# A decoder layer in two halves: early loading of the second half's weights, another order for its first batch, normalisations moved to ScalarE

## The chip, the cores and the metric

The kernel runs on one core of a Trainium2 chip. The metric is the device time of one execution in microseconds (us), as the median of several executions. The engines are TensorE (PE), VectorE (DVE), ScalarE (ACT), GpSimd (POOL) and SyncE (SP, which here only starts DMAs).

## The reference

For 16 batches of 100 rows of 512 numbers the layer computes three steps, each added to its input:

```
x = x + self_attention(layernorm(x))       # 64 heads of 32 in four windowed branches
x = x + cross_attention(layernorm(x), ctx) # 16 heads of 32, 722 context rows, top 32 scores per query
x = x + real(ifft(fft(layernorm(x)) @ w))  # as one 512x512 matrix, plus a bias
```

In the cross attention the scores are `q k / sqrt(32)`; of each query's 722 scores only the 32 largest enter the softmax, and their weights multiply the projected values. Keys and values are projections of the context (`ctx @ Wk.T + bk`, `ctx @ Wv.T + bv`). All is float32. The third step's matrix M is worked out on the chip from the spectral weights.

## The kernel before, in words

The program has two halves, each a block of five instruction streams with its own semaphores; the second starts when all engines have ended the first.

**First half** (`self_program`, L105 to L649): self attention. Each engine runs `body` for the batches -2 to 16, a software pipeline in which `cur`, `prev`, `nxt` and `far` switch stages on. While a batch's scores are computed, the q and k projections of the next one are made with the weights `WqkH` and `WqkL`, which fill the lowest part of SBUF. In the body of batch 15 nothing more is projected to q and k. SP stores `x1` to HBM (L241) and loads the residual `xres` (L239). At its end the mean row `y3` is written to HBM (L244).

**Second half** (`cross_program`, L680 to L1423): cross attention and the spectral step. It begins with a preparation:

- SP loads the signs, four folded spectral matrices and a DFT matrix in four chunks of 128 rows (L862 to L867), then the eight 128x512 pieces of the key and value weights (L869), the first half of the context (L880), the rest of the weights (`SETUP`, L886) and, after GpSimd's 16 accumulating DMAs of L912 have landed (`x1_whole`), the first batch's rows (L894).
- DVE folds each chunk (L1330, L1338), TensorE multiplies it with the DFT matrix (L1027), ACT copies the product out (L1191), and TensorE multiplies again (L1034), which ACT copies to `M` (L1305).
- ACT and DVE split the key and value weights into a high and a low part (L1195, L1349), so that three fast matmuls (`split3`, L88 to L90) stand for one exact product.

Then come the batches. A batch has 13 score tiles: 12 of 128 rows (four heads' queries for 32 numbers each, packed) and one of 64. They are worked through in seven steps, s = 0 to 6, two tiles in each and one in the last. For a tile TensorE makes the scores (`score`, into one PSUM buffer `pS`), ACT copies them to SBUF (`keep_scores`, L1246), and DVE picks the top 32: MAX8 of the scores (L1362), MATCH_REPLACE8 of the eight found (L1381), then three rounds of the same on what is left (L1372, L1384). ACT exponentiates what was there (L1239) and what was left (L1229), GpSimd subtracts (L950), TensorE transposes (L1091) and multiplies with the values (L1120, L1124). GpSimd also makes the softmax shift (L942).

Beside a batch's tiles the keys and values of the next batch are made, in 14 slices: `SLICES` lists for each half of the context four key slices and three value slices, `PLAN` says at which step each is projected by TensorE (`project`), kept by ACT (`keep`, L1215, L1219, L1221) and, for keys, given its low part by GpSimd (`key_low`, L927). Before the first batch the same plan runs with no tiles beside it. The context itself is split by ACT (L1206) and GpSimd (L935).

Two normalisations belong to a batch. At s = 0 DVE takes the statistics of the next batch's rows (`row_stats`, L95 to L97), GpSimd the inverse deviation (L997), and DVE normalises (L1394). At s = 3 DVE adds the attention's output in PSUM to the residual (L1405), takes its statistics, GpSimd makes the inverse deviation (L1000), and at s = 4 DVE normalises (L1412). Later TensorE multiplies by `M` (L1143) and DVE adds (L1417).

`settle` (L59) issues a no-operation; it stands behind many waits.

Of the kernel before, what the change touches and what calls it, by code (L numbers as in the profile page):

```python
# [17 lines left out]
F32 = mybir.dt.float32  # L18
# [86 lines left out]
def self_program(nc, A, x1_dram, y3_dram):  # L105
# [10 lines left out]
    with ExitStack() as ctx:  # L116
# [108 lines left out]
        def _(sp):  # L225
# [6 lines left out]
            def body(b, cur, prev, nxt, far):  # L232
# [447 lines left out]
def cross_program(nc, A, x1_dram, y3_dram, out_dram):  # L680
# [16 lines left out]
    assert [n for a, b in PLAN[1:] + PLAN[:1] for n in a + b] == list(range(NSL))  # L697
    with ExitStack() as ctx:
# [3 lines left out]
        chunks = lambda t, n: t.rearrange("p (c d) -> p c d", c=n)  # L702
        M = sb("M", [128, CC, D])
        WkH, WkL, WvH, WvL = (sb(n, [128, CC, D], F32R) for n in ("WkH", "WkL", "WvH", "WvL"))
# [10 lines left out]
        SLOT = [128, KV]  # L715
        KH, K32, KL, V, S = [None, None], [None, None], [None, None], [None, None], [None] * SLOTS

        def own(p):

            KH[p] = sb(f"KH{p}", [128, CC, KV], F32R)  # L720
            with ExitStack() as below:
                K32[p] = below.enter_context(nc.sbuf_tensor(f"ca_K32{p}", [128, CC, KV], F32))
            KL[p] = sb(f"KL{p}", [128, CC, KV], F32R)
            V[p] = sb(f"V{p}", [128, KC, D])

        own(0)
        with ExitStack() as below:
            fold = {n: below.enter_context(nc.sbuf_tensor(f"ca_fold_{n}", [128, CC, D], F32)) for n in FOLDS}
            dft = below.enter_context(nc.sbuf_tensor("ca_dft", [128, CC, D], F32))
            signs = below.enter_context(nc.sbuf_tensor("ca_signs", [128, CC, 4, 2], F32))  # L730
        folded, spread = fold["pp"], fold["mp"]
        own(1)
        for r in (4, 5, 6, 0, 1, 2, 3):
            S[r] = sb(f"S{r}", SLOT)

# [4 lines left out]
        W = [sb(f"W{r}", [128, KV]) for r in range(RING)]  # L740
# [6 lines left out]
        stats, mv, rstd = sb("stats", [T, 6]), sb("mv", [T, 2]), sb("rstd", [T, 1])  # L747
# [739 lines left out]
```

## Time and profile before

| | us |
|---|---|
| median of 3 runs (2321.08 to 2322.66) | 2322.45 |
| the profiled execution's own time | 2323.47 |
| its span | 2321.6 |
| DVE busy in the span | 1950.9 (84%) |
| PE busy in the span | 2076.8 (89%) |
| ACT busy | 1266.3 (55%) |
| POOL busy | 1277.2 (55%) |

Times in the rows below are us from the start of the span; the profiled execution's own time is 1.9 us more than its span, and 1.0 us more than the median. In a row of a timeline stand the start, the time from the start of the first to the end of the last instruction of the row, the engine, the line, the operation, the tiles, the shapes and the count; in brackets how long the engine was idle before it and what ended that. A row with `x2` or more merges that many instructions of one kind. SPq rows are DMA issues of SP's queue. PE's granted clock is given as a share of 2.4 GHz.

### The profile page before, as it was taken

What the parts mean: (1) busy time and instruction counts of PE and PEld (TensorE: products, weight loads), DVE (VectorE), ACT (ScalarE), POOL (GpSimd) and SP (SyncE); (2) the same over time, 40 slices, a digit from 0 to 9 for tenths busy, and PEclk for the clock granted to TensorE, in tenths of its full rate; (3) what the DMA queues carried; (4) which work ended last, traced back from release to release, by engine and by line L of the source; (5) the groups of instructions that cost most, each with busy time, mean ns of one, the idle gap of its engine ahead of it and who ended that gap; (6) DMA issues with size and microseconds to landing.
All of it is one profiled execution on the core that took longest, in us unless ns stands there. A gap on an engine that the chain in (4) does not pass through costs nothing. (4 is left out here: it accounts for less than half of the span.)

```text
span 2321.6 us, 50944 instructions
## 1 busy us (share of the span) xinstructions
PE 2076.8 (89%) x19760; PEld 1627.4 (70%) x19760; DVE 1950.9 (84%) x3662; ACT 1266.3 (55%) x2464; POOL 1277.2 (55%) x1473
## 2 busy tenths in 40 slices
PE   2899999999957889999999999999999999999966
PEld 1566666666644778787787787887878778788754
DVE  4757676676722499999999999999999999999995
ACT  4333333333312476766666666766666766666652
POOL 2555646465641465656556656556556655665642
PEclk9999999999968899999999999999999999999977
DMA  5000000000036100000001000010000000100000
GB/s 190 12 16 20 16 23 13 23 13 26 9 82 191 30 19 13 30 26 21 18 21 38 19 20 25 13 37 18 20 26 23 28 18 21 37 18 21 8 1 11
DMA packets 41501, 70.42 MB, mean 30 GB/s; under 512 B 4639, under 2 KB 21167, under 8 KB 41261
## 3 DMA queue, kind: packets, MB, share of 16 engines
q1 hardware_dynamic: 35868, 56.31, 7.8%
q0 software_dynamic: 3632, 7.58, 1.4%
q10 hardware_dynamic: 1760, 3.28, 0.5%
q8 instruction: 157, 2.57, 0.5%
q14 instruction: 84, 0.68, 0.1%
HBM read 60.54 MB, written 9.86 MB: 30 GB/s over the span
## 5 line engine op out<-in xcount | busy, mean ns | idle before, releaser
L1384 DVE MATCH_REPLACE8 ca_W<-ca_top,ca_W 128x722 f32<-128x722 f32 (+1 forms) x624 | 553.1, 892 | 0.0
L1372 DVE MAX8 ca_top<-ca_W 128x8 f32<-128x722 f32 (+1 forms) x624 | 536.8, 897 | 2.2
L950 POOL TENSOR_TENSOR ca_S<-ca_S,ca_W 128x722 f32<-128x722 f32 (+1 forms) x208 | 358.6, 1743 | 270.5 <-ACT ca_W L1229 270.5
L1229 ACT ACTIVATE ca_W<-ca_W,ca_shift 128x722 f32<-128x722 f32 (+1 forms) x208 | 185.6, 892 | 83.8 <-DVE ca_W L1384 83.7
L927 POOL TENSOR_TENSOR ca_KL<-ca_K,ca_KH 128x384 fp32r<-128x384 f32 (+1 forms) x128 | 122.7, 959 | 191.5 <-ACT ca_KH L1221 189.7
L1251 ACT ACTIVATE ca_PT<-ca_pT 128x768 f32<-128x768 f32 (+1 forms) x208 | 163.4, 786 | 105.4 <-PE ca_pT L1091 105.1
L88 PE MATMUL ca_pS<-ca_KH,ca_QH 128*128 128x362 f32 (+1 forms) x384 | 149.7, 390 | 79.1 <-ACT ca_S L1246 77.4
L1124 PE MATMUL ca_pO<-ca_PT,ca_V 128*32 128x56 f32 (+5 forms) x4608 | 216.9, 225 | 0.0
L1239 ACT ACTIVATE ca_S<-ca_S,ca_shift 128x722 f32<-128x722 f32 (+1 forms) x208 | 175.8, 891 | 60.8 <-POOL ca_shift L942 60.5
L1362 DVE MAX8 ca_top<-ca_S 128x8 f32<-128x722 f32 (+1 forms) x208 | 178.9, 897 | 28.2 <-ACT ca_S L1246 27.7
L88 PE MATMUL ca_pF<-ca_cH,ca_WkH 128*128 128x338 f32 (+1 forms) x512 | 191.8, 375 | 10.2 <-POOL ca_cL L935 9.5
L287 POOL TENSOR_TENSOR sa_ss<-sa_ss,sa_minus_half 100x16 f32<-100x16 f32 x64 | 187.1, 2941 | 20.0 <-DVE sa_ss L445 20.0
L1246 ACT ACTIVATE ca_S<-ca_pS 128x722 f32<-128x722 f32 (+1 forms) x208 | 159.1, 765 | 55.2 <-PE ca_pS L90 54.8
L1124 PEld LDWEIGHTS ca_pO<-ca_PT,ca_V 128*32 128x32 f32 x4608 | 186.2, 111 | 0.0
L1381 DVE MATCH_REPLACE8 ca_W<-ca_top,ca_S 128x722 f32<-128x722 f32 (+1 forms) x208 | 184.3, 892 | 0.0
L1091 PE MATMUL ca_pT<-ca_ident,ca_S 128*128 128x128 f32 (+1 forms) x1248 | 178.5, 280 | 0.0
L89 PE MATMUL ca_pF<-ca_cL,ca_WkH 128*128 128x338 f32 (+1 forms) x512 | 178.3, 348 | 0.0
L90 PE MATMUL ca_pF<-ca_cH,ca_WkL 128*128 128x338 f32 (+1 forms) x512 | 176.6, 345 | 0.0
L360 ACT ACTIVATE sa_E<-sa_pq 100x300 f32<-100x300 f32 x256 | 86.2, 425 | 156.5 <-PE sa_pq L90 156.5
L436 DVE TENSOR_TENSOR sa_qk<-sa_pp,sa_bias_qk 100x512 f32<-100x512 f32 x64 | 44.2, 691 | 148.0 <-PE sa_pp L90 148.0
L935 POOL TENSOR_TENSOR ca_cL<-ca_raw,ca_cH 128x768 fp32r<-128x768 f32 (+1 forms) x64 | 111.8, 1769 | 81.3 <-ACT ca_cH L1206 81.3
L276 POOL TENSOR_SCALAR_AFFINE_SELECT sa_E<-sa_E 100x400 f32<-100x400 f32 x256 | 146.6, 573 | 17.8
(212 smaller groups left out, 5178.0 us busy)
## 6 DMA issues: line engine op xcount, KB each, us to landing
ca_raw<-in_ctxT SPq DMA_DIRECT2D x32, 384.0 KB, 4.2
ca_raw<-in_ctxT SPq DMA_DIRECT2D x32, 338.0 KB, 3.0
sa_xin<-in_x SPq DMA_DIRECT2D x16, 200.0 KB
sa_xres<-in_x SPq DMA_DIRECT2D x16, 200.0 KB
x_scratch<-sa_x SPq DMA_DIRECT2D x16, 200.0 KB
x_scratch<-y_scratch POOLq DMA_DIRECT2D x16, 200.0 KB, 15.1
ca_xin<-x_scratch SPq DMA_DIRECT2D x16, 200.0 KB
ca_x<-x_scratch SPq DMA_DIRECT2D x16, 200.0 KB
```

The costliest lines, as they stand in the source:

```text
L88: pe.matmul(out, ah, bh, start=start, stop=False)
L89: pe.matmul(out, ah, bl, start=False, stop=False)
L90: return pe.matmul(out, al, bh, start=False, stop=stop)
L287: pool.tensor_tensor(part, part, minus_half[:, 0:NH], ALU.pow).then_inc(norm_ready, 1)
L950: pool.tensor_tensor(S[k][rows, :], S[k][rows, :], W[r][rows, :], ALU.subtract).then_inc(p_ready, 1)
L1091: last = pe.transpose(pT[:, 128 * k:128 * k + t.rows], S[slot(t)][0:t.rows, KEY0[k]:KEY0[k] + 128], ident[0:t.rows, 0:t.rows])
L1124: last = pe.matmul(pO[to:to + DH, NUM + at + q.start:NUM + at + q.stop], V[tp][:, k, 128 * g + to:128 * g + to + DH], PT[:, k, cols], star ...
L1229: act.activation(W[r][rows, :], W[r][rows, :], ACT.Exp, bias=shift[rows, r:r + 1], scale=SCALE).then_inc(f_ready, 1)
L1362: dve.max(top[r][rows, 0:8], S[slot(t)][rows, :]).then_inc(peaked, 1)
L1372: n_of[t.i] = order.mark(dve.max(top[r][rows, 8 * k:8 * k + 8], W[r][rows, :]))
L1381: dve.match_replace(W[r][rows, :], eight, S[slot(t)][rows, :], REMOVED).then_inc(removed, 1)
L1384: ins = dve.match_replace(W[r][rows, :], eight, W[r][rows, :], REMOVED)
```

## The change

It does four things.

1. A class `Early` owns the folded matrices, the DFT matrix, the signs and eight buffers for the key and value weights. They lie where the first half has `WqkH` and `WqkL`. SP loads them (29 DMAs) in the body of the first half's batch 15, when all q and k projections have been done. In SP's order they stand ahead of the wait for `x1` of batch 14, its store, and the load of `xres` for batch 15. The second half's SP stream begins with the context and `SETUP`.
2. ACT splits the key and value weights first and copies the spread matrices afterwards.
3. The first batch has its own plan: all eight key slices first (five before the first score, three between the first two scores) and the six value slices in step 0 of the batch, between its scores. The second context half gets buffers of its own (`cH0`, `cL0`). For this batch DVE makes the low parts of the context and of the queries instead of GpSimd, and ACT makes the high part of the queries at s = 2. The output bias is made in batch 0 at s = 2 (PE) and s = 3 (DVE).
4. ACT normalises, as `rstd * x + center`, where `center` = -mean * rstd is one more small GpSimd operation. ACT copies the attention's output from PSUM to SBUF, and GpSimd adds it to the residual. DVE's statistics of step 3 come one round later. All `settle` calls but one are gone.

```diff
+class Early:
+        with ExitStack() as below:
+            sb = lambda n, s: below.enter_context(nc.sbuf_tensor("early_" + n, s, F32))
+            self.fold = {n: sb("fold_" + n, [128, CC, D]) for n in FOLDS}
+            self.dft, self.signs = sb("dft", [128, CC, D]), sb("signs", [128, CC, 4, 2])
+            self.staged = [sb(f"staged{u}", [128, D]) for u in range(2 * CC)]
+    def load(self, sp):
+        sp.dma_start(self.signs[:, :, :, :], A["fold_signs"]).then_inc(self.signs_in, 16)
+        for c in range(CC):
+            for n in FOLDS:
+                sp.dma_start(self.fold[n][:, c, :], A["W" + n][rows, :]).then_inc(self.fold_in[c], 16)
+            sp.dma_start(self.dft[:, c, :], A["dft"][rows, :]).then_inc(self.fold_in[c], 16)
+        for u in range(2 * CC):
+            sp.dma_start(self.staged[u][:, :], A[w][128 * c:128 * c + 128, :]).then_inc(self.w_in, 16)
...
                     sp.dma_start(xres[:, :], batch_of(A["x"], b, -1)).then_inc(xres_in, 16)
+                    if cur and not nxt:
+                        sp.wait_ge(qk_mm, QB * B)
+                        early.load(sp)
                     sp.wait_ge(x1_ready, b.count(1, 0))
...
+    FIRST_SLICES = sorted(SLICES, key=lambda x: x[1])
     PLAN = [([12], [13]), ([], [0, 1]), ([2], [3]), ([4, 5], [6]), ([], [7, 8, 9]), ([10], []), ([], [11])]
+    FIRST_PLAN = [([8, 9, 10], [11, 12, 13]), ([], [0, 1]), ([2], [3]), ([4], []), ([], []), ([], []), ([5, 6, 7], [])]
...
+            def scales(done):
+                order.after(order.mark(pool.tensor_tensor(rstd[:, :], mv[:, 1:2], minus_half[:, :], ALU.pow)))
+                pool.tensor_scalar(center[:, :], mv[:, 0:1], rstd[:, :], -1.0, ALU.mult, ALU.mult).then_inc(done, 1)
...
+                    if s == 3 and prev:
+                        pool.wait_ge(y_kept, b.count(1, 0))
+                        pool.wait_ge(xb_ready, b.count(1, 0))
+                        pool.tensor_tensor(x2[:, :], x2[:, :], xin[:, :], ALU.add).then_inc(x2_ready, 1)
...
+                    if s == 4 and prev:
+                        act.wait_ge(rstd2_ready, b.count(1, 0))
+                        act.activation(xin[:, :], x2[:, :], ACT.Identity, bias=center[:, 0:1],
+                                       scale=rstd[:, 0:1]).then_inc(xn2_ready, 1)
                     for x in cur:
                         exps(*x)
+                    if s == 0 and nxt:
+                        act.wait_ge(rstd1_ready, bn.count(1, 1))
+                        act.activation(xin[:, :], xin[:, :], ACT.Identity, bias=center[:, 0:1],
+                                       scale=rstd[:, 0:1]).then_inc(xn1_ready, 1)
...
+                    if s == 2 and prev:
+                        act.wait_ge(x1T_mm, bn.count(1, 1) if nxt else b.count(1, 1) if tiles else b.count(1, 0))
+                        act.wait_ge(y_mm, b.count(1, 0))
+                        act.activation(xin[:, :], pX[0:T, :], ACT.Copy).then_inc(y_kept, 1)
...
-                        if k == 3 and s == 0 and nxt:
-                            dve.wait_ge(rstd1_ready, bn.count(1, 1))
-                            dve.tensor_scalar(xin[:, :], xin[:, :], mv[:, 0:1], rstd[:, :],
-                                              ALU.subtract, ALU.mult).then_inc(xn1_ready, 1)
-                        if k == 0 and s == 3 and prev:
-                            dve.tensor_tensor(x2[:, :], pX[0:T, :], x2[:, :], ALU.add).then_inc(x2_ready, 1)
+                        if k == 1 and s == 3 and prev:
                             dve.wait_ge(x2_ready, b.count(1, 0))
                             row_stats(dve, order, x2[:, :], stats[:, :], mv[:, :], var2_ready)
-                        if k == 0 and s == 4 and prev:
-                            dve.tensor_scalar(xin[:, :], x2[:, :], mv[:, 0:1], rstd[:, :],
-                                              ALU.subtract, ALU.mult).then_inc(xn2_ready, 1)
```

## Rows read from the trace of the kernel before

**Rows 1.** The page's busy time of each engine over the whole span.
```profile
PE 2076.8 (89%) x19760; PEld 1627.4 (70%) x19760; DVE 1950.9 (84%) x3662; ACT 1266.3 (55%) x2464; POOL 1277.2 (55%) x1473
```

**Rows 2.** Busy time of PE, PEld, DVE, ACT, POOL by stretch, granted clock, DMA.
```profile
676.00:741.00 65.00, 32.53 (x70) 13.90 (x70) 20.41 (x42) 10.78 (x19) 21.70 (x25) 0.78 0.79 222
741.00:786.30 45.30, 39.61 (x189) 35.12 (x189) 1.60 (x2) 16.46 (x32) 15.58 (x16) 0.86 0.11 33
...
876.00:2206.00 1330.00, 1249.67 (x11051) 1057.15 (x11048) 1321.13 (x2353) 904.66 (x1689) 785.07 (x900) 0.97 0.08 23
```

**Rows 3.** DVE's groups by line, 876 to 2206 us: count, busy, mean ns.
```profile
L1394 DVE TENSOR_SCALAR ca_xin<-ca_xin,ca_mv,ca_rstd 100x512 f32<-100x512 f32 x14 | 16.1, 1150 | 0.0
...
L1405 DVE TENSOR_TENSOR ca_x<-ca_pX,ca_x 100x512 f32<-100x512 f32 x14 | 9.5, 681 | 0.0
...
L1412 DVE TENSOR_SCALAR ca_xin<-ca_x,ca_mv,ca_rstd 100x512 f32<-100x512 f32 x14 | 8.6, 614 | 0.0
```

**Rows 4.** DVE's timeline at step 3 of a middle batch.
```profile
1297.17 1.72 DVE L1362 MAX8 ca_top<-ca_S 128x8 f32<-128x722 f32 x2
...
1300.55 0.68 DVE L1405 TENSOR_TENSOR ca_x<-ca_pX,ca_x 100x512 f32<-100x512 f32 x1
1301.34 0.69 DVE L95 BATCH_NORM_STATS2 ca_stats<-ca_x 100x6 f32<-100x512 f32 x1
```

**Rows 5.** GpSimd's timeline at steps 3 and 4 of that batch.
```profile
1301.94 0.40 POOL L942 TENSOR_SCALAR ca_shift<-ca_top 128x1 f32<-128x1 f32 x2
...
1317.75 1.28 POOL L1003 TENSOR_TENSOR ca_x<-ca_x,ca_bias_f 100x512 f32<-100x512 f32 x1
```

**Rows 6.** SP's DMA issues between the halves.
```profile
679.02 0.36 SPq L862 DMA_DIRECT2D ca_signs<-in_fold_signs  x1
...
711.58 0.90 SPq L880 DMA_DIRECT2D ca_raw<-in_ctxT  x2
...
723.84 1.21 SPq L894 DMA_DIRECT2D ca_xin<-x_scratch  x1
```

**Rows 7.** Timeline of the preparation: GpSimd, DVE and PE.
```profile
679.45 14.08 POOL L912 DMA_DIRECT2D x_scratch<-y_scratch  x16 [24.09 <-POOLq L116]
...
691.04 1.97 DVE L1330 TENSOR_SCALAR ca_fold_pp<-ca_fold_pp,ca_signs 128x257 f32<-128x257 f32 x1 [14.08 <-DMA ca_dft<-in_dft]
...
695.62 5.28 PE L1027 MATMUL ca_acc<-ca_dft,ca_fold_pp 128*128 128x512 f32 x8 [19.38 <-DVEq L1343]
...
700.14 0.35 DVE L1330 TENSOR_SCALAR ca_fold_pp<-ca_fold_pp,ca_signs 128x257 f32<-128x257 f32 x1 [4.63 <-DMA ca_dft<-in_dft]
...
721.72 13.90 PE L1034 MATMUL ca_acc<-ca_fold_mp,ca_dft 128*128 128x512 f32 x32
```

**Rows 8.** Timeline of the first batch's projections, up to DVE's second MAX8.
```profile
740.68 0.69 PE L88 MATMUL ca_pF<-ca_cH,ca_WkH 128*128 128x384 f32 x1 [4.71 <-POOL ca_cL L935]
...
747.67 3.71 PE L1177 MATMUL ca_pX<-ca_xT,ca_WqT 128*128 128x100 f32 x32
...
767.53 0.60 ACT L1215 ACTIVATE ca_V<-ca_pF 128x512 f32<-128x512 f32 x1 [2.19 <-PE ca_pF L90]
...
780.48 0.54 ACT L1219 ACTIVATE ca_K<-ca_pF,ca_bk 128x338 f32<-128x338 f32 x1 [0.82 <-PE ca_pF L90]
...
786.35 0.91 DVE L1362 MAX8 ca_top<-ca_S 128x8 f32<-128x722 f32 x1 [1.20 <-ACT ca_S L1246]
```

**Rows 9.** Batch 0, step 4: its second tile's scores kept, and DVE's MAX8 of both.
```profile
834.21 0.78 ACT L1246 ACTIVATE ca_S<-ca_pS 128x722 f32<-128x722 f32 x1 [0.17 <-PE ca_pS L90]
...
841.66 1.71 DVE L1362 MAX8 ca_top<-ca_S 128x8 f32<-128x722 f32 x2
```

**Rows 10.** DVE in the first half's end: the last q/k projection's bias, and the last residual.
```profile
620.02 0.69 DVE L436 TENSOR_TENSOR sa_qk<-sa_pp,sa_bias_qk 100x512 f32<-100x512 f32 x1 [1.84 <-PE sa_pp L90]
...
672.84 0.69 DVE L477 TENSOR_TENSOR sa_x<-sa_pw,sa_xres 100x512 f32<-100x512 f32 x1 [5.63 <-PE sa_pw L579]
```

**Rows 11.** ACT copying 512 columns of PSUM.
```profile
735.66 0.60 ACT L1305 ACTIVATE ca_M<-ca_acc 128x512 f32<-128x512 f32 x1 [0.26 <-PE ca_acc L1034]
```

More of the change, by code:

```diff
@@ L854, in slices, with plan_of, slice_of, context_of @@
             if s == 0:
-                return [(b, par, n) for n in PLAN[s][part]] if tiles else []
-            return [(b.next(), 1 - par, n) for n in PLAN[s][part]] if nxt else []
+                return [(b, par, n) for n in plan_of(b)[s][part]] if tiles else []
+            return [(b.next(), 1 - par, n) for n in plan_of(b.next())[s][part]] if nxt else []
+        def plan_of(b):
+            return PLAN if b.const else FIRST_PLAN
+        def slice_of(b, n):
+            return (SLICES if b.const else FIRST_SLICES)[n]
+        def context_of(b, half):
+            return (cH, cL) if b.const or half == 0 else (cH0, cL0)
         block = ctx.enter_context(nc.Block())
@@ L1042, in project @@
             def project(bn, pn, n):
-                half, kind, k = SLICES[n]
+                half, kind, k = slice_of(bn, n)
                 k0, kn = HALVES[half]
-                if n % 7 == 0:
+                if n % 7 == 0 or not bn.const and n == 4:
                     pe.wait_ge(ctx_lo, bn.count(4, 2 * half + 2))
                 need(pe, kv_out, bn.count(NSL, n - 1))
+                cH, cL = context_of(bn, half)
                 for c in range(CC):
@@ L1155, in body @@
                         score(*coming[1])
-                    if s == 2 and not tiles and nxt:
-                        pe.wait_ge(q_ready, CC)
+                    if s == 2 and tiles and not prev:
+                        pe.wait_ge(q_ready, bn.count(CC, CC))
                         for c in range(CC):
@@ L1161, in body @@
                         ins.then_inc(bias_mm, 1)
-                    if s == 0 and tiles and not prev:
-                        pe.wait_ge(bias_ready, 1)
                     if s == 2 and prev:
@@ L1188, in _ @@
         def _(act):
+            act.wait_ge(early.w_in, 16 * len(WSPLIT))
+            for u, (wh, _, c) in enumerate(WSPLIT):
+                act.activation(wh[:, c, :], early.staged[u][:, :], ACT.Copy).then_inc(w_hi, 1)
             for c in range(CC):
@@ L1355, in body @@
                     n_of = {}
+                    if s == 0 and not tiles and nxt:
+                        first_context_low(bn, 0)
+                        first_context_low(bn, 1)
                     for tb, tp, t in cur:
@@ L1429, in program @@
     y3_dram = nc.dram_tensor("y3_scratch", (B, D), F32, kind="Internal").ap()
-    self_program(nc, A, x1_dram, y3_dram)
-    cross_program(nc, A, x1_dram, y3_dram, out)
+    with ExitStack() as ctx:
+        early = Early(nc, A, ctx)
+        self_program(nc, A, early, x1_dram, y3_dram)
+        cross_program(nc, A, early, x1_dram, y3_dram, out)
 def kernel(**inputs):
```

188 lines of the change are left out of this document (99 added, 89 removed).

## The prediction

> **What bounds the kernel now.** I read the page's busy times first, then the busy time by stretch, then DVE's groups, then timelines. The page alone misleads: PE is busy 89% and DVE 84% [rows 1]. By stretch it is otherwise. From 876 to 2206 us, 14 batches of 95.0 us each, DVE is busy 1321.13 of 1330 us, 99.3%, and its groups have no idle time before them; PE is busy 94.0% there with modelled ends [rows 2, 3]. So the batches are bound by DVE, and whatever leaves its stream shortens each by its own length. Between the halves DVE does next to nothing: 20.41 us of work in 676 to 741 and 1.60 in 741 to 786.3 [rows 2]. There first DMAs, then TensorE set the pace: DVE waited 14.08 us for the first chunk [rows 7], 29 early loads took SP from 679.02 to 711.58 [rows 6], and the second MAX8, from which DVE never stops again, began at 786.35 [rows 8]. The kernel's time is thus that moment, plus DVE's work, plus a tail.
>
> **DVE's stream, per batch.** Three instructions leave it. L1394 takes 1.15 us in the mean; neighbours overlap by 0.1 (a MAX8 takes 0.91, two stand in 1.72), so 1.05 [rows 3, 4, 8]. L1412: 0.61 less 0.1, 0.51 [rows 3]. L1405 and the statistics behind it start 0.79 apart [rows 4]; all of that goes, since the statistics then wait for another engine: 0.79. Sum 2.35 us. Each has 16 executions, but one of L1394 lies before the first batch and one of the others in the tail: 15 x 2.35 = 35.3 us. The removed no-operations: the only gap beside one is in these 0.79, already counted (0.79 - 0.68 = 0.11); elsewhere pairs follow without a gap. I take them at nothing; the bounds are 0 and 0.11 us at some three lone instructions of the 64-row tile, 5 us in all.
>
> What replaces them. ACT gets two normalisations and a copy. The nearest row is its 512-column copy, 0.60 us [rows 11], so 1.8 us a batch on an engine that is busy 904.66/1330 = 68% [rows 2]. GpSimd gets the addition, like L1003 1.28 us [rows 5], and two small `center` operations like half of L942's pair, 0.2 each: 1.7 us at 59% busy. Both have room on average; what counts is where they stand. In ACT's stream, `exps` of the step and everything behind wait 0.6 us longer at s = 0 and s = 4, and GpSimd's subtraction needs them only a step later. ACT's copy of the output waits for TensorE's output product, but the value or key slice behind it would have made ACT wait for a later TensorE instruction anyway. At s = 3 GpSimd's addition stands behind the shifts, so no exponential waits for it.
>
> The tight place is DVE's statistics at s = 3, now a round later. A step's round is 1300.55 - 1297.17 = 3.38 us [rows 4], so DVE asks for `x2` at 1297.17 + 6.76 = 1303.93. GpSimd ends the shifts at 1301.94 + 0.40 = 1302.34 and the addition at 1303.62, plus 0.05 for the semaphore: 1303.67 [rows 5]. The margin is 0.26 us. The bounds are 0 and, were GpSimd late by the whole addition, 1.28 us a batch; I take 0.07, 1 us in all, because the one margin I can compute is positive.
>
> A batch would take 95.0 - 2.35 + 0.07 = 92.7 us. PE has 5.7 us a batch not busy [rows 2], so it needs no more than it can give.
>
> **The early loads.** They can begin when the last q/k projection is done, just before 620.02 [rows 10]. Issuing the 29 took 32.6 us before, under full load [rows 6], so SP is free at about 653 and the data is in well before the second half starts at 679.0. Queued behind them on SP are the store of batch 14's `x1` and the load of the last `xres`; who waits is DVE's L477 at 672.84 [rows 10]. That leaves 20 us for two small transfers, so this costs nothing; if each issue took 1.7 us instead of 1.1, the cover would be gone and each further us would be paid once. DMA traffic beside compute: 0 to 1 us, I take 0.
>
> **From 679.0 to the first projection.** DVE folds at once. The first chunk took 695.62 - 691.04 = 4.6 us, of which L1330 1.97; without GpSimd beside it L1330 took 0.35, so a chunk is 3.0 [rows 7]. GpSimd issues its 16 accumulating DMAs until 679.45 + 14.08 = 693.5, [rows 7], so I give three chunks the long form: ready at 683.6, 688.2, 692.8, 695.8. PE's eight matmuls take 5.3 us at the start, when its clock is low [rows 7], and 13.90/32 x 8 = 3.5 at the high one: 688.9, 692.4, 696.3, 699.8. Then ACT's copies stay beside PE, and the second product, 13.9 us, ends at 713.8. It ended at 735.6 before [rows 7]: 21.8 us.
>
> Beside it run the weight splits on DVE (from 700.4, eight of 0.6, done 705.5), the context's high part on ACT (1.6) and low part on DVE (two of 0.9), done at 709; GpSimd needed until 740.68 for it [rows 8]. The row load waits for GpSimd's accumulated rows: issued at 723.84 before [rows 6], behind `SETUP`. Now the queue ahead of it is a third as long. I take 705 for the data, so statistics, two GpSimd operations and ACT's normalisation are done by 712; bounds 705 to 720. First projection at 714.4 instead of 740.68: 26.3 us.
>
> The Trainium skill has a rule that speaks against this part. Its page "SBUF — State Buffer", section "Who interferes with whom", says that a DMA from GpSimd's queue needs GpSimd to write descriptors, and that a DVE instruction holding both ports in its fast mode locks it out for the instruction's length. The trace agrees on one side of it: L1330, a fast-mode kind, took 1.97 us while GpSimd worked and 0.35 alone [rows 7]; how much GpSimd lost, no row shows. What it would do here is rival 3.
>
> **From the first projection to DVE's start.** Value slices are spaced 0.60 + 2.19 = 2.8 us; key slices of 338 columns 1.9 (0.54 + 0.82 and the 0.5 copy between), of 384 columns by width 2.15 [rows 8]. Before, 45.7 us led from 740.68 to 786.35: eight keys, three values, the queries, the bias, a 4.8 us wait for the context's second half, and some 30 matmuls at low clock. Now: 4 x 2.15 + 4 x 1.9 = 16.2, queries 3.5, two scores of 1.1 (2.11 between two MAX8, less the 0.8 copy [rows 8]), the last copy with semaphores 0.9. The clock is high, because PE comes straight from 14 us of work. New waits: ACT does the context and 2.5 us of query copies ahead of keeping slice 2, so slice 4 waits 1.4 us; and the first score waits for slice 4's copy, rounding and low part, 2.2. Sum 26.4: the second MAX8 begins at 740.8 instead of 786.35, 45.5 us earlier. Bounds: waits of 0 to 10 us more, so 36 to 49.
>
> **What it costs behind.** In step 0 PE has six value slices instead of three, hence 8.4 us more; with the score that stands behind them I take 9.5 us by which the next batch's context and projections come later relative to DVE. The bias product, 3.5 us, comes in too. Before, in step 4 the second tile's scores were there at 834.99 and needed at 842.5: 7.5 us early [rows 9]. Delay 9.5 + 3.5 = 13 less 7.5 and less 3 that PE wins back from its own waits: 2.5. I take 3 (0 to 8), and 0.6 for the bias addition in DVE's stream.
>
> **The tail.** L1405 with its gap, 0.79 [rows 4], becomes ACT's copy 0.60, GpSimd's addition 1.28 and two semaphores 0.1; `center` adds 0.25. Total +1.5 us.
>
> **Sum** from the profiled execution's own 2323.47: -45.5 + 3 + 0.6 - 35.3 + 1 + 1.5 = -74.7, so 2248.8; the median of the runs lies 1.0 lower, 2247.8. I say 2248.
>
> **Rivals.**
> 1. A wait takes the place of the work removed: DVE waits for GpSimd's addition in each batch. For it: a margin of 0.26 us, with GpSimd's subtraction ahead of it depending on ACT, which now has more to do. Against: ACT was idle before that step. Price 1.28 x 15 less the 1 counted: +18, 2266. Chance 0.09.
> 2. The first batch stalls: value slices behind the scores cost what they saved. For: 6 slices where PE already had no gap. The whole 8.4 us of the extra slices and the bias show, 12 instead of 3.6: 2256. Chance 0.12.
> 3. GpSimd's DMAs are held back by the folding. If all 11.8 us of it came on top, they would be issued at 705 and landed several us later; rows, statistics and normalisation would follow, and the projections would start about 12 us late: 2260. Against: the fast-mode instructions are only four. Chance 0.07. (By the rule on locks alone, four times 0.35 us, nothing would change.)
> 4. Slower than before: TensorE becomes the limit and its clock falls. Place: the batches. PE's work is 0.94 x 95 = 89.3 us at a granted clock of 0.97; it would take more than 92.7 from a clock of 0.93 on. The start and tail gain 40.4, or 2.7 us for each of 15 batches, so the kernel is slower only if a batch takes over 97.7, at a mean clock under 0.89. At 0.87 a batch takes 99.6: 2323.5 - 40.4 + 69 - 1 = 2351. For: stretches with gaps on PE show 0.78 and 0.86 [rows 2]. Against: the batches have fewer gaps than before. Chance 0.03.
> 5. The early loads don't do what is said: they are still landing at 679, or the first half's end waits for SP. Price up to 12: 2260. Chance 0.03.
>
> The forecast has 0.66. 2232 to 2266 holds it with the bounds above (start 36 to 49 with stall 0 to 8, no-operations up to 5) and reaches over all but rival 4. A measurement can tell 0.2%, 4.6 us, from no change. Faster: all but rival 4, 0.96; within 0.2%: 0.01; slower: 0.03.
>
> **What would show it.** No DMA wait ahead of L1330's first instruction at about 679; the second product ending near 714; the second MAX8 near 741; DVE still 99% busy in the batches and their period 92.7 us; in step 3 no idle time ahead of DVE's statistics (rival 1 would show over 1 us); idle time ahead of MAX8 in batch 0 of about 3 us; a tail 1.5 us longer. I am wrong if the period stays at 95 or DVE idles in each batch, or if the first projection comes later than 725.

## The result, and the profile after

The changed kernel took 2260.69 us in the median of four executions (2254.43 to 2261.72), the kernel before 2321.76 on the same chip; the ratio is 0.9733, 95% interval 0.9713 to 0.9752. The forecast was 2248 with a range of 2232 to 2266. The sign and most of the size were right; 12.7 us of the gain did not come. The profiled execution took 2261.72 us, 12.9 more than the 2248.8 forecast from the profiled one.

The page's busy row and three stretches of the changed kernel (PE, PEld, DVE, ACT, POOL busy, granted clock, DMA share, GB/s):

```profile
PE 2057.5 (91%) x19760; PEld 1605.7 (71%) x19760; DVE 1922.3 (85%) x3623; ACT 1291.4 (57%) x2512; POOL 1288.7 (57%) x1512
```
```profile
676.00:741.00 65.00, 52.21 (x173) 29.65 (x171) 29.35 (x51) 21.03 (x41) 22.60 (x28) 0.91 0.56 135
741.00:786.00 45.00, 39.08 (x195) 35.46 (x196) 34.20 (x63) 21.29 (x37) 14.90 (x18) 0.92 0.07 21
876.00:2136.00 1260.00, 1197.32 (x10704) 1006.92 (x10703) 1246.40 (x2238) 902.04 (x1688) 787.57 (x920) 0.99 0.08 23
```

Against [rows 1, 2]: DVE lost 28.6 us of work and is still the limit of the batches (98.9% busy); 741 to 786, in which it did 1.60 us before, holds 34.20. PE is 95.0% busy in the batches and its granted clock rose from 0.97 to 0.99. It did not become the limit.

Three moments divide the difference: DVE's last addition of the first half, its second MAX8, and the end. First the kernel before, then the changed one; the row at 788.93 and its like are the statistics of the next batch's rows, one a batch:

```profile
676.28 0.68 DVE L481 TENSOR_TENSOR sa_xn<-sa_pp,sa_bias_o 16x512 f32<-16x512 f32 x1 [2.75 <-PE sa_pp L585]
...
788.93 0.68 DVE L95 BATCH_NORM_STATS2 ca_stats<-ca_xin 100x6 f32<-100x512 f32 x1
...
879.87 0.68 DVE L95 BATCH_NORM_STATS2 ca_stats<-ca_xin 100x6 f32<-100x512 f32 x1
...
2107.51 0.68 DVE L95 BATCH_NORM_STATS2 ca_stats<-ca_xin 100x6 f32<-100x512 f32 x1
```
```profile
682.58 0.68 DVE L511 TENSOR_TENSOR sa_xn<-sa_pp,sa_bias_o 16x512 f32<-16x512 f32 x1 [2.75 <-PE sa_pp L615]
...
694.44 5.00 DVE L1383 TENSOR_SCALAR early_fold_pp<-early_fold_pp,early_signs 128x257 f32<-128x257 f32 x1
...
719.86 0.69 DVE L95 BATCH_NORM_STATS2 ca_stats<-ca_xin 100x6 f32<-100x512 f32 x1 [1.97 <-DMA ca_xin<-x_scratch]
...
752.64 0.92 DVE L1436 MAX8 ca_top<-ca_S 128x8 f32<-128x722 f32 x1 [6.92 <-ACT ca_S L1280]
...
755.22 0.68 DVE L95 BATCH_NORM_STATS2 ca_stats<-ca_xin 100x6 f32<-100x512 f32 x1
...
811.86 0.91 DVE L1436 MAX8 ca_top<-ca_S 128x8 f32<-128x722 f32 x1 [2.54 <-ACT ca_S L1280]
...
849.93 0.68 DVE L95 BATCH_NORM_STATS2 ca_stats<-ca_xin 100x6 f32<-100x512 f32 x1
...
897.77 0.69 DVE L95 BATCH_NORM_STATS2 ca_stats<-ca_x 100x6 f32<-100x512 f32 x1 [2.40 <-POOL ca_x L1032]
...
990.31 0.69 DVE L95 BATCH_NORM_STATS2 ca_stats<-ca_x 100x6 f32<-100x512 f32 x1 [0.69 <-POOL ca_x L1032]
...
2051.07 0.68 DVE L95 BATCH_NORM_STATS2 ca_stats<-ca_xin 100x6 f32<-100x512 f32 x1
```

- The first half ends 6.3 us later (682.58 against 676.28).
- From there to the second MAX8 it is 70.06 us instead of 110.07 (786.35, [rows 8]): -40.0. The part up to the end of the second product fell from 59.3 to 36.9 us, the part behind it from 50.7 to 33.2.
- From the second MAX8 to the end of the span, 1507.3 instead of 1535.25: -28.0.

The sum is -61.7, the difference of the spans (2259.9 and 2321.6). A batch took 94.4 us in the mean before (13 periods from 879.87 to 2107.51) and takes 92.4 after (849.93 to 2051.07). The idle times in brackets are the new waits: 2.54 us in the first batch (0.75 and 0.63 at two other places), and GpSimd's addition of `x2`, for which DVE waits 2.40 us once and 0.54 to 0.95 in seven later batches, 7.2 in all. In the fold DVE's scaling instruction L1383 comes once a chunk; the first three took 0.35 to 0.36 us, the fourth 5.00.

TensorE at the end of the first half, before and after the change: eight matmuls at the high clock, and the same eight behind an idle stretch, at a granted clock of 0.83 in 633 to 643 us:

```profile
632.71 3.60 PE L528 MATMUL sa_pp<-sa_Wv,sa_xT 128*100 128x512 f32 x8
```
```profile
635.55 0.45 PE L587 MATMUL sa_pt<-sa_rden,sa_ident 32*32 32x100 f32 x10 [2.39 <-issue]
...
637.10 5.29 PE L558 MATMUL sa_pp<-sa_Wv,sa_xT 128*100 128x512 f32 x8
```

TensorE and SP at the start of the second half of the changed kernel:

```profile
705.58 13.90 PE L1069 MATMUL ca_acc<-early_fold_mp,early_dft 128*128 128x512 f32 x32
...
722.98 0.90 PE L1098 MATMUL ca_pX<-ca_ident,ca_xin 100*128 100x100 f32 x4 [3.50 <-ACT ca_xin L1343]
```
```profile
691.04 3.38 SPq L917 DMA_DIRECT2D ca_bias_f<-in_ffn_bias  x1
...
716.79 0.28 SPq L923 DMA_DIRECT2D ca_xin<-x_scratch  x1
```

The second product ended at 719.5, where the forecast (713.8 plus the 6.3) put it. Then TensorE waited 3.50 us for the first normalised rows: SP stood 22.4 us, 694.4 to 716.8, waiting for GpSimd's 16 accumulating DMAs.

### The profile page after: what moved, and what is told of

Its sections match the earlier page's. It is cut to its first block, busy times and chain, and to the rows that moved or that the text cites. A ratio compares the mean times of both kernels' runs of the same rounds, so it can differ in the third digit from the quotient of the medians.

```text
span 2259.9 us, 50468 instructions
## 1 busy us (share of the span) xinstructions
PE 2057.5 (91%) x19760; PEld 1605.7 (71%) x19760; DVE 1922.3 (85%) x3623; ACT 1291.4 (57%) x2512; POOL 1288.7 (57%) x1512
## 4 chain that ended last, share of the span: by engine, by line
DVE 37%; PE 18%; issue 8%; ACT 3%; POOL 2%; DMA 1%; POOLq 0%; DVEq 0%; ACTq 0%
DVE ca_top L1445 15%; DVE ca_W L1456 14%; DVE ca_W L1453 3%; DVE ca_top L1436 3%; PE ca_pF L88 2%; PE ca_pF L89 2%; PE ca_pF L90 2%; PE ca_pT L1126 2%; PE ca_pO L1158 2%; PE ca_pX L1211 2%; PE ca_pX L1203 1%; PE ca_pS L88 1%; DMA x_scratch<-y_scratch 1%; ACT ca_W L1263 1%; PE ca_pS L90 1%
## 5 line engine op out<-in xcount | busy, mean ns | idle before, releaser
L1158 PE MATMUL ca_pO<-ca_PT,ca_V 128*32 128x28 f32 (+5 forms) x4608 | 216.9, 225 | 0.0
L88 PE MATMUL ca_pF<-ca_cH,ca_WkH 128*128 128x338 f32 (+1 forms) x512 | 185.2, 362 | 7.4 <-ACT ca_K L1253 7.1
L89 PE MATMUL ca_pF<-ca_cL,ca_WkH 128*128 128x338 f32 (+1 forms) x512 | 170.9, 334 | 0.0
L90 PE MATMUL ca_pF<-ca_cH,ca_WkL 128*128 128x338 f32 (+1 forms) x512 | 170.8, 334 | 0.0
L90 PE MATMUL ca_pF<-ca_WvH,ca_cL 128*128 128x512 f32 x384 | 151.1, 394 | 0.0
```

The source lines that it names most:

```text
L88: pe.matmul(out, ah, bh, start=start, stop=False)
L89: pe.matmul(out, ah, bl, start=False, stop=False)
L90: return pe.matmul(out, al, bh, start=False, stop=stop)
L1158: last = pe.matmul(pO[to:to + DH, NUM + at + q.start:NUM + at + q.stop], V[tp][:, k, 128 * g + to:128 * g + to + DH], PT[:, k, cols], star ...
```

## The experiments

Each ran beside the kernel before; ratios are against it. Executions of one kernel differ by up to 10.6 us (2316.73 to 2327.37 for nine of the kernel before), so where a few us matter I compare stretches of the profiles: F, the last addition of the first half; M, the second MAX8; E, the end of the span. The changed kernel has M - F = 70.1 and E - M = 1507.3. E - M ends in a tail whose length goes with TensorE's clock: from the end of the last search instruction to E it is 28.3 to 32.9 us in the fourteen profiles, 31.1 before and 29.6 in the changed kernel. Where that matters, S stands for the end of the last search instruction; S - M is 1477.7 in the changed kernel.

**The changed kernel again.** No edit.

> The changed kernel itself, run again beside the variants. Theory: its four times lay 7.3 us apart (2254.43 to 2261.72) because single batches of the first half take 1 to 4 us longer in some executions, so the profiled first half ends somewhere between 676.3 and 682.6 us, and the median lies between 2254 and 2262. Rival: the 6.3 us by which the first half ended later come with the change; then DVE's addition at the first half's end stands at 682 to 683 us again, and PE again has an idle stretch of about 2.4 us while the early loads run.

2262.01 us (2259.92 to 2265.04), 0.9742 [0.9726, 0.9757]. F at 682.06, M - F 69.7, E - M 1508.2, and PE's idle stretch again, 2.22 us. The x2 waits came three times (2.40, 1.80, 1.75) instead of eight; their sum, 6.0, is nearly the same.

**Early loads issued in the second half.** 

```diff
-                    if cur and not nxt:
-                        sp.wait_ge(qk_mm, QB * B)
-                        early.load(sp)
...
         def _(sp):
+            early.load(sp)
```

> The changed kernel, but the 29 early loads are issued at the start of the second half. Theory (the loads are worth about what the fold waited for): the first half ends at 676 to 678.5 us as in the kernel before, the second product's end moves back to 733 to 736, and the kernel is 14 us slower than the changed one (about 2274): of the fold's 14.1 us wait for its first chunk all comes back, less the 4.2 us that the loads cost the first half, plus the setup loads queued behind them on SP. Rival (row load, not fold, sets the first projection): the first projection hardly moves against the changed kernel's, and the difference is under 6 us.

2279.90 us (2279.43 to 2281.04), 0.9817 [0.9803, 0.9832]: 17.9 slower than the changed kernel beside it. DVE waited 13.94 us for the first chunk and PE its 19.5:

```profile
678.14 0.68 DVE L508 TENSOR_TENSOR sa_xn<-sa_pp,sa_bias_o 16x512 f32<-16x512 f32 x1 [2.75 <-PE sa_pp L612]
...
692.76 2.25 DVE L1382 TENSOR_SCALAR early_fold_pp<-early_fold_pp,early_signs 128x257 f32<-128x257 f32 x1 [13.94 <-DMA early_dft<-in_dft]
...
771.35 0.91 DVE L1435 MAX8 ca_top<-ca_S 128x8 f32<-128x722 f32 x1 [7.28 <-ACT ca_S L1279]
```

M - F is 93.2, 23 us more, of which F gives 4 back. The theory's 14 was too small: it counted only the first chunk's wait, and the later chunks (DVE waits 4.93, 7.02 and 2.38 us more, PE 2.47 and 6.17) and the setup behind them come on top. The rival is out.

So 23 of the 40 us at the start are the loads. The next experiment but one gives 7 to the order of the slices. If the parts add, some 10 are left, for ACT's new order and for the low parts that DVE makes instead of GpSimd; no run takes these back. The trace points at the low parts: in the kernel before, TensorE stood 4.71 us [rows 8] and 4.82 us for GpSimd's low part of the context, and the changed kernel has neither wait. Before:

```profile
772.31 0.65 PE L88 MATMUL ca_pF<-ca_cH,ca_WkH 128*128 128x338 f32 x1 [4.82 <-POOL ca_cL L935]
```

**Normalisations back on DVE.** DVE gets L1394, L1405 and L1412 of the kernel before at their old places; GpSimd's `center` and x2 addition and ACT's three instructions go.

```diff
-                        if k == 1 and s == 3 and prev:
-                            dve.wait_ge(x2_ready, b.count(1, 0))
+                        if k == 0 and s == 3 and prev:
+                            dve.wait_ge(y_mm, b.count(1, 0))
+                            dve.wait_ge(xb_ready, b.count(1, 0))
+                            dve.tensor_tensor(x2[:, :], pX[0:T, :], x2[:, :], ALU.add).then_inc(x2_ready, 1)
+                            dve.wait_ge(x2_ready, b.count(1, 0))
...
```

> The changed kernel with the two normalisations and the x2 addition back on DVE, GpSimd's center operations and ACT's copy of y gone. Theory: every batch is longer by the 2.35 us that left DVE's stream less the 0.48 us a batch that DVE waits for GpSimd's addition: +1.9 x 15 = 28 us, and the tail is as much as 1.5 us longer; about 2289. Rival: part of the 2.25 us by which the period shrank comes from the removed no-operations; then the period here stays below 94.0 us and the kernel is under 22 us slower. DVE's waits of 0.6 to 2.4 us ahead of the statistics should be gone in both.

2285.58 us (2283.44 to 2288.41), 0.9843 [0.9826, 0.9859]: 23.6 slower. In the profiles E - M is 1534.9, 27.6 more than the changed kernel's, as expected (28); F, 677.40 there by chance since the first half is untouched, gives 4.7 of it back. DVE's waits for GpSimd at step 3 are gone. The shortest period, the first two of each profile left out, is 93.89 us, against 94.17 before and 91.75 after. So this part is worth 2.14 us a batch gross, and the rival keeps 0.3 of the 2.42: its period under 94.0 came, its kernel under 22 us slower did not.

**The first batch's slices in the old order.**

```diff
-    FIRST_SLICES = sorted(SLICES, key=lambda x: x[1])
+    FIRST_SLICES = SLICES
-    FIRST_PLAN = [([8, 9, 10], [11, 12, 13]), ([], [0, 1]), ([2], [3]), ([4], []), ([], []), ([], []), ([5, 6, 7], [])]
+    FIRST_PLAN = PLAN
-                if n % 7 == 0 or not bn.const and n == 4:
+                if n % 7 == 0:
```

> The changed kernel with the first batch's slices in the old order (keys and values of the first half of the context, then of the second) and at the old steps. Theory: three value slices of 2.8 us and their waits come back ahead of the first scores, so the second MAX8 is 12 to 20 us later than 752.6 (the first scores wait for the second context half too), the 3.9 us of stalls in the first batch go, and the kernel is 10 to 16 us slower. Rival: the wait for the second half of the context sets the time of the first scores in either order, then under 5 us.

2259.85 us (2257.09 to 2261.09), 0.9730 [0.9714, 0.9745]: the same as the changed kernel within what can be measured, where 10 to 16 us slower was expected. M - F is 76.9, 7 us more. But no MAX8 in the first batch waits, the first x2 wait falls from 2.40 to 0.22, and E - M is 1500.0, 7.3 less. Both theories fail in the sum: the new order brings the second MAX8 forward, and the same time is lost again behind it.

**First row alone.**

```diff
-            for i in range(B):
-                pool.dma_start(x1_dram[i], y3_dram[i:i + 1, :].broadcast_to((T, D)), accum_op=ALU.add).then_inc(x1_whole, 16)
+            pool.dma_start(x1_dram[0], y3_dram[0:1, :].broadcast_to((T, D)), accum_op=ALU.add).then_inc(x1_first, 16)
...
                         scales(rstd1_ready)
+                        if not tiles:
+                            for i in range(1, B): ...
...
-                    sp.wait_ge(x1_whole, 16 * B)
+                    sp.wait_ge(x1_first, 16)
```

> The changed kernel, but GpSimd issues only the first batch's accumulating DMA ahead of its memsets, the first row load waits for that one alone, and the other 15 are issued after the first batch's scale. Theory (the 15 DMAs and the setup loads behind them hold the row): TensorE no longer has its 3.5 us idle stretch ahead of the first transposes, the fold's fourth fast instruction falls from 5.0 to about 0.36 us, and the second MAX8 comes 3 to 5 us earlier relative to the end of the first half; the kernel is about 3 us faster than the changed one, if batch 0 does not give it back. Rival (SP's own queue or the setup transfers hold it): the row lands no earlier than 34 us after the first half's last store, and nothing changes.

2251.09 us (2250.31 to 2253.55), 0.9698 [0.9680, 0.9715]. Its F was early (677.92), so of the 10 us only part is the edit; M - F is 63.4, 6.6 less, and E - M 1507.2, the same. GpSimd and PE:

```profile
681.09 0.99 POOL L942 DMA_DIRECT2D x_scratch<-y_scratch  x1 [24.47 <-POOLq L143]
...
710.29 13.28 POOL L1032 DMA_DIRECT2D x_scratch<-y_scratch  x15
```
```profile
699.71 13.47 PE L1074 MATMUL ca_acc<-early_fold_mp,early_dft 128*128 128x512 f32 x31
...
713.01 0.51 PE L1103 MATMUL ca_pX<-ca_ident,ca_xin 100*128 100x100 f32 x4
```

The transposes follow the product without a gap, and no fold instruction takes over 1.58 us (beside GpSimd's memsets). 3.5 us are the row and 1.6 the fold (the second product ends 35.3 us behind F instead of 36.9); the rest goes with TensorE's clock: after its 3.50 us stretch the first slice's matmuls took 0.52 us each in the changed kernel, 0.34 here.

**GpSimd's x2 addition first.** The `if s == 3 and prev:` block with the addition moves ahead of `weights`, `inverse` and `shifts`.

> The changed kernel with GpSimd's x2 addition of step 3 ahead of its subtractions, inverses and shifts of that step. Theory: DVE's waits ahead of the x2 statistics (2.40 us in batch 0, 0.54 to 0.95 us in about every second later batch, 7.2 us in all) vanish, the batches' period is 91.8 us in all batches, and the kernel is 5 to 7 us faster. Rival: the addition is then late for its own inputs, the output product and ACT's copy, and holds the shifts: DVE waits as long elsewhere, 0 us.

2258.84 us (2254.91 to 2261.45), 0.9728 [0.9709, 0.9747], inconclusive as a time. All waits for x2 in the batches went, yet E - M stayed at 1507.0. Part of that is the tail, 32.5 us here: S - M is 1474.6, 3.1 less. But 7.2 us of waits went. Periods of 92.0 to 92.5 us remained with no idle time in them. The difference is DVE's small product for the last tile; its group from 860 to 2140 us, first in the changed kernel, then in this one:

```profile
L1468 DVE TENSOR_TENSOR ca_ctxT<-ca_NR 32x64 f32<-32x64 f32 x14 | 3.6, 258 | 0.4
```
```profile
L1468 DVE TENSOR_TENSOR ca_ctxT<-ca_NR 32x64 f32<-32x64 f32 x14 | 8.5, 605 | 0.4
```

and one such case, with GpSimd's subtraction that began 0.14 us earlier:

```profile
1147.85 0.94 DVE L1468 TENSOR_TENSOR ca_ctxT<-ca_NR 32x64 f32<-32x64 f32 x1
```
```profile
1147.71 1.00 POOL L955 TENSOR_TENSOR ca_KL<-ca_K,ca_KH 128x384 fp32r<-128x384 f32 x1 [2.71 <-ACT ca_KH L1255]
```

DVE's instruction, 0.22 us alone, ends with GpSimd's, at 1148.79 and 1148.71. It is no single case: of its 16 executions here the 12 that began while GpSimd was in a `tensor_tensor` took 0.25 to 0.95 us and ended 0.08 to 0.09 us behind GpSimd's end, and the 4 that met none took 0.22. So 4.9 of the 7.2 us came back as a longer instruction, which no view of waits shows.

**No-operations back in DVE's stream** (three `settle(dve)` calls).

> The changed kernel with the no-operations back in DVE's stream ahead of the first-round maxima and replacements. Theory: with the normalisations back on DVE a period without waits was 93.93 us against 94.21 in the kernel before, so the no-operations are worth 0.28 us a batch: +4 us, the shortest periods 92.0. Rival: they cost nothing; then the shortest periods stay at 91.75.

2260.66 us (2259.55 to 2265.44), 0.9741 [0.9722, 0.9760]: no difference. The shortest periods are 91.83 us, 0.08 more. By that the no-operations were worth about 1 us in all, and S - M (1477.4) shows not even this; 0.2 us a batch between the kernel before and the one with the normalisations on DVE stays unexplained.

**Output bias product early.** TensorE's four matmuls and DVE's addition move ahead of the first transposes.

```diff
+                        if not tiles:
+                            for c in range(CC):
+                                ins = pe.matmul(pX[0:T, :], bv[:, c:c + 1].broadcast_to((128, T)), WoT[:, c, :], ...)
+                            ins.then_inc(bias_mm, 1)
+                            pe.wait_ge(bias_ready, 1)
```

> The changed kernel with the output bias product (3.5 us of TensorE) and DVE's addition of it moved from the first batch's steps 2 and 3 to the time in which TensorE waits for the first normalised rows. Theory (TensorE's backlog makes the stalls of the first batch): the first transposes come 0.5 to 1.5 us later, and the stalls of batch 0 and the first x2 wait, 6.3 to 7.7 us in the two executions seen, fall by 3 us or more; 2 to 3 us faster. Rival (the stalls come from waits between the engines, not from the amount of work): the stalls stay within 1 us and the kernel is 1 us slower.

2257.22 us (2255.06 to 2260.32), 0.9723 [0.9705, 0.9742], with its F 2 us late (684.53). M - F 69.5, E - M 1504.4, 2.9 less: the 2.54 us stall is gone, the others (0.73, 1.93) stay, and so does the first x2 wait (2.40). Stalls and first wait together are 5.1 us against 6.3 and 7.7 in the two profiles of the changed kernel, so they fell by less than the theory's 3. TensorE's amount of work makes the 2.54 us stall; the others it does not explain.

**The last tile's product on GpSimd**, with the addition first.

```diff
+                if t.rest:
+                    pool.drain()
+                    pool.wait_ge(o_kept, tb.count(GROUPS, n + 1))
+                    pool.wait_ge(ot_ready, tb.count(GROUPS, n))
+                    rest = [chunks(NR[3 * DH:128, i, 0:4 * REST], 4) for i in range(2)]
+                    pool.tensor_tensor(ctxT[3 * DH:128, :, T - REST:T], rest[0], rest[1], ALU.mult).then_inc(ot_ready, 1)
...
-                        if k == 3 and s == 1 and prev:
...
```

> As the variant with GpSimd's x2 addition first, and besides DVE's small product of the last tile's output (32x64) is done by GpSimd. Theory: with the addition first, DVE's waits of 7.2 us went, but that product took 605 ns in the mean instead of 258, up to 0.95, ending when GpSimd's subtraction beside it ended: the two engines' fast instructions exclude each other, and the gain was given back there. Without it in DVE's stream the periods are 91.5 us nearly throughout and the kernel is 8 to 11 us faster than the changed one. Rival: the given-back time was chance, or GpSimd in its turn comes late (it drains and waits for its own result there); then the sum of the batches is within 3 us of the changed kernel's.

2248.53 us (2247.62 to 2249.06), 0.9678 [0.9665, 0.9691]: 12 to 13.5 faster than the changed kernel, some 4 of it an early F (678.00). S - M is 1465.6, 12.1 less than the changed kernel's and 9.0 less than with the addition first alone, where the product took DVE 8.5 us. Eleven of its periods are 91.36 to 91.38 us; two waits for scores (0.64, 1.25) are left in the later batches. With E - M 9.6 less the forecast of 8 to 11 us came true, and GpSimd did not come late. That the two engines exclude each other is shown by the ends of the instructions above; this run shows what the lengthened one cost.

**Three combinations.** All have the first row alone, the early bias product, the addition first and the last tile's product on GpSimd, and issue the early loads behind batch 14's `x1` store. The first keeps the new order, the second has the old one, the third puts slices 5 to 7 behind both scores (`([], [5, 6, 7])` in step 6).

> All that helped, together: first row alone first, bias product early, x2 addition first, the last tile's product on GpSimd, and besides the early loads issued behind the x1 store of the first half's last full batch. Theory: gains add up, 7 + 3 + 10 us below the changed kernel, so about 2241; and TensorE's idle stretch of 2.1 to 2.6 us in the first half, seen in all seven executions with early loads 13 to 15 us after their first issue and in none without, moves with the loads (to about 662 us) or goes where no new instructions are fetched. Rival: the stretch stays at 631 to 636 us; then it is not the loads' doing.

> The same, with the first batch's slices in the order of the kernel before. Theory: the order moves TensorE's work but removes none, so from the end of the first half to the third batch's statistics it takes as long as the new order (262.4 against 261.6 and 262.7 us in the executions so far), and the two kernels are within 2 us. Rival: with the bias product out of the way the new order stalls less and is 4 us or more faster.

> The same as with the new order, but the three later key slices stand behind the second score instead of between the first and the second. Theory: the second MAX8 comes 5 to 6 us earlier, and the first batch stalls by as much more, because TensorE's work up to the third score is the same: within 2 us of the new order. Rival: the first step's 13.5 us of maxima cover it; 4 us or more faster.

They took 2245.06 us (2241.26 to 2245.86), 0.9660 [0.9645, 0.9675]; 2242.54 (2241.32 to 2243.54), 0.9652 [0.9639, 0.9666]; and 2243.94 (2240.53 to 2249.47), 0.9668 [0.9650, 0.9687]. In these times the order of the slices makes no difference that can be told. From F to S the profiles have 1530.9, 1533.2 and 1529.9 us, so the old order may be 2 to 3 us behind here, where it was level in the changed kernel (1547.2 against 1547.7). With the old order DVE has no idle time at all in the batches; the statistics of the third batch's rows and of the last's:

```profile
844.90 0.68 DVE L95 BATCH_NORM_STATS2 ca_stats<-ca_xin 100x6 f32<-100x512 f32 x1
...
2032.73 0.68 DVE L95 BATCH_NORM_STATS2 ca_stats<-ca_xin 100x6 f32<-100x512 f32 x1
```

That is 13 periods of 91.37 us. The gains of the first combination did not quite add up, 2241 was expected: once the rows come early, the bias product finds no wait of TensorE to hide in and pushes the transposes back. In the first combination they begin 40.7 us behind F, with the first row alone 35.1:

```profile
715.39 3.60 PE L1199 MATMUL ca_pX<-ca_WoT,ca_bv 128*100 128x512 f32 x8
...
719.77 0.39 PE L1111 MATMUL ca_pX<-ca_ident,ca_xin 100*128 100x100 f32 x2 [0.78 <-DVE ca_bias_o L1478]
```

By these two a version with the bias product left in the first batch may start sooner; it was not tried, and there the 2.54 us stall would come back.

In these three, PE's idle stretch at 631 to 636 us is gone; with the loads issued from 645 us on, 0.57 to 0.69 us is left at 665 to 666. It was 2.05 to 2.62 us in all nine profiles whose loads began near 620 (the expectation above says seven; there were eight when it was written), and absent in the two without loads there. The idle stretch is thus the loads' doing. The page lists TensorE's instructions as a DMA queue of their own on the same engines; that their fetch is what came late is a guess that no run tested apart.

What the loads cost the first half is less plain. From the last batch's first DVE reduction to F the profiles have:

| | idle stretch | short stretches at half clock that begin at 633 to 647 us | to F, us |
|---|---|---|---|
| before | none | none | 69.8 |
| loads in the second half | none | one | 71.5 |
| loads near 620, four profiles | 2.05 to 2.35 | none | 71.9 to 72.0 |
| loads near 620, four profiles | 2.06 to 2.62 | one | 73.8 to 74.3 |
| loads near 620, early bias product | 2.12 | two | 75.7 |
| the three combinations | 0.57 to 0.69 | one | 72.4 to 72.5 |

Line against line, one such stretch of low clock goes with 1.4 to 2.4 us more, the idle stretch with 2.1 to 2.8. The nine have a mean of 73.3, 2.7 above that of the two without loads, but some of this is the clock, which fell in the kernel with no loads there as well. Whether the loads make it fall more often, two profiles on one side can't tell.

## Why the prediction was right, and what it missed

The second MAX8 came at 752.64 instead of 740.8: 6.3 us from the first half, 2.9 from the row, 2.6 from the path behind it. From there to the end 29.2 us less were forecast and 28.0 measured. Together that is the 12.9 us. That the second figure is so close is in part luck: up to the last search instruction 30.7 less were forecast and 26.4 measured, and the tail, by TensorE's clock, gave 3 us back. The forecast also took a batch for 95.0 us, 14 in 1330 us; the rows of the statistics give 94.4.

**The start: -45.5 us at the second MAX8 forecast, -33.7 measured.** The waits for the early data are gone, as forecast: no DMA wait ahead of the fold, first and second product on time to 1 us. Three terms were mis-sized.
- "DMA traffic beside compute: 0 to 1 us, I take 0." The first half ended 6.3 us later. 2.4 us of it is TensorE's stretch during the loads, 1.7 the low clock behind it (5.29 us for eight matmuls instead of 3.60), and 1.7 one more batch of 38.9 instead of 37.2 us; such batches, each with a short stretch at half clock, are in both kernels (two before, three after). So the change answers for the first, perhaps for the second, and nothing ties it to the third. The forecast weighed the transfers' time, not what they share.
- The row. "I take 705 for the data", 711.3 with the late F; it came at 719.86 and cost 2.9 us at the first projection. It was late because SP waits for all 16 accumulating DMAs, and these moved among 4.3 MB that SP loads: in 684 to 725 the DMA engines gave 45.8% of their time to the one queue and 34.5% to the other. Rival 3 named the place, and the wrong culprit. GpSimd issued its 16 DMAs in 14.24 us, as before (14.08, [rows 7]): folding did not hold it back. By the Trainium skill ("SBUF — State Buffer", "Who interferes with whom") a DVE instruction in its two-port mode and GpSimd exclude each other, and whichever issues first holds the ports while the other is blocked. The trace agrees on the side on which DVE is blocked, 5.00 us instead of 0.36 in the fold; the prediction told only the other side, on which GpSimd is.
- The path from the first projection to the second MAX8: 26.4 forecast, 29.1 measured. The clock was not high at its start, since TensorE did not come straight from its product but from the 3.50 us wait: 0.52 us for a matmul that takes 0.34 later, which is 1.0 us over the first two slices. The clock fell once more at 743 us, with 0.49 for 0.32.

**The first batch: 3 forecast, 3.9 measured** (5.3 in the repeat). The mechanism and size were right. What the forecast never did was set it against what the order gains: the old order loses 7 us at the second MAX8 and wins 7.3 behind it. Of the parts that a run took back (the loads, the order, the normalisations) this one brought nothing; rival 2's thought, that the slices behind the scores cost what they saved, was true of the order itself, though not at its price of 12.

**DVE's stream: 2.35 us a batch forecast.** The shortest period fell from 94.17 to 91.75, 2.42. Undoing the part alone costs 2.14. The mean period fell by 2.04 against 2.28 forecast with the x2 wait taken off. Its largest term, L1394 with 1.15 us, was an instruction of 0.54 us lengthened by GpSimd's work beside it, as L1468 is: in the kernel before 10 of its 16 executions took 1.05 to 1.89 us, each ending 0.28 to 0.29 us behind one of GpSimd's context subtractions (L935), and the other 6 took 0.53 to 0.55. L1412, the same operation on the same shape, takes 0.55 in the tail. One long and one short case:

```profile
1362.88 1.87 DVE L1394 TENSOR_SCALAR ca_xin<-ca_xin,ca_mv,ca_rstd 100x512 f32<-100x512 f32 x1
...
1457.84 0.54 DVE L1394 TENSOR_SCALAR ca_xin<-ca_xin,ca_mv,ca_rstd 100x512 f32<-100x512 f32 x1
```

**The x2 wait: 1 forecast, 7.2 measured.** This is the step that failed in kind. The margin of 0.26 us was read off one batch. In the third batch of the changed kernel DVE asks for the result at 989.62 (990.31 less its 0.69 us wait), and GpSimd's addition, behind its subtractions, inverses and shifts, ends at 990.28:

```profile
988.99 1.29 POOL L1032 TENSOR_TENSOR ca_x<-ca_x,ca_xin 100x512 f32<-100x512 f32 x1
```

By its price of 18 us rival 1 (chance 0.09) was 40% true. The first batch's backlog pays into it as well: 2.40 us with the new order, 0.22 with the old.

**The tail: +1.5 forecast, -1.5 measured** (from the last search instruction, 32.0 to 30.5). The last tile's chain has the added operations: from the output product's start to the final addition 17.77 us after, 17.62 before, with a product of 5.08 instead of 6.71, so +1.8: the forecast's mechanism and size hold, and the -1.5 is the clock. TensorE's granted clock in the last 50 us falls to half in different places. In the four profiles in which its mean from 40 to 20 us before the end is 0.50 to 0.59, the time from the last search to the end is 32.1 to 32.9 us; in the other ten, with 0.61 to 0.78, it is 28.3 to 31.1. This tail can't be forecast to better than that.

**TensorE as the limit** (rival 4) did not happen: the granted clock of the batches rose from 0.97 to 0.99.

## What to carry to other kernels

Work moved off the limiting engine pays its full length only if the engine that takes it is early in every batch: read the margin over many batches, and put the hand-over ahead of that engine's other work. Moving work behind the first result of a busy engine gained nothing here, where the engine had the same work to do before the first undisturbed batch; look at the time from start to the first undisturbed batch, not to the first result. A prefetch should be looked at for what else uses the DMA engines at both ends, and the one transfer that the chain waits for deserves its own semaphore.

## What the runs showed of the hardware

- Some DVE instructions that meet GpSimd at work do not wait in view but last longer: a 32x64 product takes 0.22 us alone and up to 0.95, ending when GpSimd's instruction ends; a 100x512 normalisation 0.54 and up to 1.89; in the fold 0.36 became 5.00 beside GpSimd's DMA issue and memsets. It counts as busy. Not all do: the addition L1405, one operand of which is in PSUM, took 0.68 to 0.69 us in all 16 executions, 15 of them beside GpSimd. With the product on GpSimd (8.5 us of DVE's time) the undisturbed periods are 91.36 to 91.38 us.
- TensorE stood 2.05 to 2.62 us in each of nine profiles during some 300 GB/s of loads that it does not use, not at all in the two without them, and 0.6 to 0.7 us with the same loads 25 us later.
- One short stretch of TensorE at half clock made a first-half batch 1.7 us longer (38.9 for 37.2), in the kernel before as in the changed one.
- No-operations in DVE's stream, 39 a batch, cost 0.08 us a batch in the shortest periods.
